# Third convolution: offset taps from TensorE to VectorE, turned values copied by ScalarE

## The reference

```
q   = dwconv3x3(x, stride 1)                       # queries, 16x16
k   = dwconv3x3(x, stride 2)                       # keys, 8x8
v   = dwconv3x3(x, stride 1)                       # values, 16x16
off = dwconv3x3(x, stride 2)                       # offsets, 8x8
off = gelu(layernorm(off) * ln_g + ln_b)
pos = tanh(reference points + w_off2 @ off)        # one (y, x) for each of 64 positions
v'  = bilinear samples of v at pos                 # 64 values
out = w_out @ attention-like product of q, k and v' (scores are not normalised by a softmax)
x   = x + out
```

## Time and profile before

| | |
|---|---|
| device time, median of three runs | 1309.3 us |
| device time of the profiled execution | 1304.56 us |
| span of the profiled execution | 1302.5 us, mean granted TensorE clock 0.947 |
| TensorE matmul (PE) busy | 1172.8 us, 90% |
| TensorE weight load (PEld) busy | 1019.4 us, 78% |
| VectorE (DVE) busy | 808.1 us, 62% |
| ScalarE (ACT) busy | 483.3 us, 37% |
| GpSimd (POOL) busy | 251.7 us, 19% |
| L1613, value taps | 64 operations, 64.6 us |
| L1781, query taps | 144 records, 66.5 us |

### The profile page before, as it was taken

The page is one execution under the profiler, slowest core; times in us unless marked ns, Lnnn a source line. Parts: engine busy times, 40 slices in busy tenths (PEclk is TensorE's granted clock), DMA queues, the critical chain, the costliest instruction groups (busy, mean ns, idle before and its releaser), DMA issues. The chain is left out here.

```text
span 1302.5 us, 23938 instructions
## 1 busy us (share of the span) xinstructions
PE 1172.8 (90%) x8436; PEld 1019.4 (78%) x8436; DVE 808.1 (62%) x2931; ACT 483.3 (37%) x944; POOL 251.7 (19%) x233
## 2 busy tenths in 40 slices
PE   2979999957999999999999999999999997997776
PEld 1968888946999998888897767678888986886455
DVE  6136676746667664666675676655767667677556
ACT  3524333313555553333332223233333322232452
POOL 3002212122010100311121343332121213111200
PEclk9989999977999999999998999999999999999677
DMA  3301000010000000000000000000000000000000
GB/s 134 83 9 62 17 30 19 1 49 1 2 2 1 2 1 2 1 1 0 0 1 1 2 2 1 2 2 1 2 0 0 1 1 1 1 1 4 1 10 36
DMA packets 11561, 15.67 MB, mean 12 GB/s; under 512 B 7385, under 2 KB 9007, under 8 KB 11346
## 3 DMA queue, kind: packets, MB, share of 16 engines
q1 hardware_dynamic: 10754, 12.86, 3.1%
q10 hardware_dynamic: 720, 1.66, 0.3%
HBM read 11.37 MB, written 3.15 MB: 11 GB/s over the span
## 5 line engine op out<-in xcount | busy, mean ns | idle before, releaser
L943 PEld LDWEIGHTS moe_dn<-all_w,moe_hid 128*128 128x128 f32 x2304 | 269.9, 192 | 5.4
L943 PE MATMUL moe_dn<-all_w,moe_hid 128*128 128x96 f32 x2304 | 271.7, 275 | 0.0
L878 ACT ACTIVATE moe_hid<-moe_up 128x512 f32<-128x512 f32 x288 | 169.9, 599 | 230.8 <-PE moe_up L935 218.3
L933 PE MATMUL moe_up<-front_xh,front_w1h 97*128 97x512 f32 x288 | 122.0, 424 | 0.7 <-PEq L1474 0.4
L935 PE MATMUL moe_up<-front_xl,front_w1h 97*128 97x512 f32 x288 | 113.7, 395 | 0.0
L827 DVE SCALAR_TENSOR_TENSOR all_X<-moe_dn,front_gate,all_X 128x96 f32 (+1 forms) x384 | 95.2, 310 | 29.4 <-PE moe_dn L943 24.6
L934 PE MATMUL moe_up<-front_xh,front_w1l 97*128 97x512 f32 x288 | 113.1, 393 | 0.0
L819 DVE SCALAR_TENSOR_TENSOR all_X<-all_b,front_gate,all_X 128x96 f32 (+1 forms) x384 | 102.6, 329 | 14.0 <-DVE all_X L827 7.6
L1371 PE MATMUL l1c_o<-l1c_vs,l1c_pt 128*128 128x64 f32 x768 | 94.4, 277 | 0.5 <-DVE l1c_ro L1149 0.5
L1371 PEld LDWEIGHTS l1c_o<-l1c_vs,l1c_pt 128*128 128x128 f32 x768 | 91.8, 195 | 2.9 <-issue 0.9
L1115 DVE TENSOR_REDUCE l1c_nmax<-l1c_sc 128x2 f32<-128x512 f32 x96 | 61.8, 686 | 40.1 <-PE l1c_sc L1338 39.4
(11 more groups left out here) (393 smaller groups left out, 2038.8 us busy)
## 6 DMA issues: line engine op xcount, KB each, us to landing
all_w<-w SPq DMA_DIRECT2D x3, 582.0 KB
all_w<-w SPq DMA_DIRECT2D x3, 576.0 KB
all_X<-x_rows SPq DMA_DIRECT2D x2, 768.0 KB, 6.9
conv_scratch<-all_X SPq DMA_DIRECT2D x2, 768.0 KB, 3.2
all_X<-conv_scratch SPq DMA_DIRECT2D x2, 768.0 KB, 4.9
out_tokens<-l3f_y SPq DMA_DIRECT2D x5, 288.0 KB, 2.1
l0c_band<-band ACTq DMA_DIRECT2D x1, 1248.0 KB, 9.4
all_b<-b SPq DMA_DIRECT2D x3, 192.0 KB
```

Of the source, the lines that this page charges most:

```text
L878: act.activation(hid[:, n, :], up[n % UPS][:, :], ACT.Gelu).then_inc(hid_done, 1)
L933: pe.matmul(bank, w1h[:, n, :], xh[:, p, :], start=True, stop=False)
L943: last = pe.matmul(dn[e % 2][:, j * C:(j + 1) * C], hid[:, n, j * P:(j + 1) * P], w2[:, n, :], start=(k == 0), stop=(k == KC - 1))
```

## The change

The nine offset taps go from TensorE to VectorE. They read `xp` at stride two in rows and columns, for both images at once: 17 rows of 8 elements, 136 elements in 96 partitions; the row between the two images is of no use. Tap 0 is a `tensor_scalar` with factor and bias, taps 1 to 8 are `scalar_tensor_tensor` operations with the running sum as second input, each waiting for the one before. TensorE turns the result by two ordinary matmuls with the identity (64 positions each) in place of one transpose. This turn now stands after the keys' taps and the turn of the values. VectorE's copy of the turned values is made by ScalarE, after the two score copies. `diag` has two kinds left of three, so GpSimd makes one fewer in the stage before. Keys and queries stay on TensorE.

```diff
-        self.diag = s.sb("diag", [C, 3, KS * KS, C])
+        self.diag = s.sb("diag", [C, 2, KS * KS, C])
...
-        for w in (2, 1, 0):
+        for w in (1, 0):
...
-        off = s.sb("off", [C, KP2])
+        off = s.sb("off", [C, KROWS, KSIDE])
...
+            def offset_taps(p, lo, hi):
+                if lo == 0:
+                    wait(dve, S["xp_done"], p + 1)
+                    wait(dve, S["on_in"], p)
+                for t in range(lo, hi):
+                    dy, dx = t // KS, t % KS
+                    rows = xp[:, p % 2, dy:dy + 2 * KROWS - 1:2, dx:dx + SIDE:2]
+                    if t == 0:
+                        ins = dve.tensor_scalar(off[:, :, :], rows, taps[:, 2, 0:1], bias[:, 2:3], ALU.mult, ALU.add)
+                    else:
+                        ins = dve.scalar_tensor_tensor(out=off[:, :, :], in0=rows, scalar=taps[:, 2, t:t + 1],
+                                                       in1=off[:, :, :], op0=ALU.mult, op1=ALU.add)
+                    if t < TAPS - 1:
+                        chain.sync(ins)
+                    else:
+                        ins.then_inc(S["off_done"], 1)
...
             for p in range(NP + 2):
+                if live(p):
+                    offset_taps(p, 0, 5)
                 if live(p - 2):
                     add_output(p - 2, 0)
                 if live(p):
-                    value_taps(p, 1, 5)
+                    offset_taps(p, 5, TAPS)
+                    value_taps(p, 1, 4)
                 if live(p - 2):
                     add_output(p - 2, 1)
                 if live(p):
                     offset_moments(p)
-                    value_taps(p, 5, 6)
+                    value_taps(p, 4, 6)
                     offset_norm(p)
-                if live(p - 1):
-                    values_out(p - 1)
...
-            def offsets_out(p):
-                wait(act, S["off_in"], p + 1)
-                wait(act, S["on_in"], p)
-                act.activation(off[:, :], off_ps, ACT.Identity, bias=bias[:, 2:3]).then_inc(S["off_out"], 1)
+            def values_out(p):
+                wait(act, S["vt_in"], p + 1)
+                wait(act, S["vb_in"], 2 * p)
+                act.activation(vt[:, :, :, :].rearrange("p i t c -> p (i t c)"), vp[:, 0:4 * C], ACT.Copy
+                               ).then_inc(S["vt_out"], 1)
...
                 if live(p - 1):
                     scores_out(p - 1, 0)
                     scores_out(p - 1, 1)
+                    values_out(p - 1)
...
-            def conv_offsets(p):
-                wait(pe, S["xp_done"], p + 1)
-                wait(pe, S["th_done"], p)
-                conv(off_ps, 2, p, 2, 0, TAPS).then_inc(S["off_in"], 1)
...
             def turn_offsets(p):
-                wait(pe, S["off_out"], p + 1)
-                pe.transpose(on_ps, off[:, :], ident[0:C, 0:C]).then_inc(S["on_in"], 1)
+                wait(pe, S["off_done"], p + 1)
+                wait(pe, S["th_done"], p)
+                for i in range(2):
+                    o = off[:, PAD // 2 * i:PAD // 2 * i + KSIDE, :].rearrange("c y x -> c (y x)")
+                    ins = pe.matmul(on_ps[KPIX * i:KPIX * (i + 1), :], o, ident[0:C, 0:C], start=True, stop=True)
+                ins.then_inc(S["on_in"], 1)
...
             for p in range(NP + 1):
-                if live(p):
-                    conv_offsets(p)
                 if p == NP - 1:
+                    pe.wait_ge(S["xp_done"], NP)
                     F.pe_turn(pe)
...
                 if live(p):
-                    turn_offsets(p)
                     conv_keys(p)
...
                 if live(p - 1):
                     turn_values(p - 1)
                 if live(p):
+                    turn_offsets(p)
                     conv_queries(p, 0, 4)
```

More of the change, by code:

```diff
@@ L1469, in l2_conv @@
     ROWS = PAD + SIDE
+    KROWS = PAD // 2 + KSIDE
     BATCHES = ((0, 8), (8, 20), (20, NT))
@@ L1500, in l2_conv @@
         k_ps, y_ps = ky[0:C, 0:KP2], ky[:, KP2:KP2 + 2 * C]
-        off_ps, on_ps, og_ps, pos_ps = fp[0:C, 0:KP2], fp[:, KP2:KP2 + C], fp[0:C, KP2 + C:KP2 + C + P], fp[:, 0:2 * KP2]
+        on_ps, og_ps, pos_ps = fp[:, 2 * KP2:2 * KP2 + C], fp[0:C, 2 * KP2 + C:2 * KP2 + C + P], fp[:, 0:2 * KP2]
         vb_ps = vb[0:BLK, 0:4 * C]
         names = ("tap_done", "var_done", "rstd_done", "dve_step", "xn_done", "turned",
-                 "xp_done", "off_in", "off_out", "on_in", "ovar_done", "orstd_done", "on_done", "og_in", "og_out",
+                 "xp_done", "off_done", "on_in", "ovar_done", "orstd_done", "on_done", "og_in", "og_out",
                  "pos_in", "th_done", "dist_done", "hat_done", "bil_done", "val_done", "vt_in", "vt_out", "k_in", "k_out",
@@ L1618, in value_taps @@
                         ins.then_inc(S["val_done"], 1)
[L1620 to L1624, removed]
             def sampled_out(p, i):
@@ L1743, in _ @@
             for p in range(NP + 1):
-                if live(p):
-                    offsets_out(p)
                 if p == NP - 1:
@@ L1783, in conv, with conv_keys @@
                 return ins
-            def conv_offsets(p):
+            def conv_keys(p):
                 wait(pe, S["xp_done"], p + 1)
-                wait(pe, S["th_done"], p)
-                conv(off_ps, 2, p, 2, 0, TAPS).then_inc(S["off_in"], 1)
-            def conv_keys(p):
                 wait(pe, S["k_out"], p)
```

## The result

| | before | after |
|---|---|---|
| device time, median (range, runs) | 1307.79 us (1304.84 to 1318.88, 4) | 1341.95 us (1337.88 to 1343.05, 4) |
| ratio, with its 95% interval | | 1.0239 (1.0195 to 1.0283) |
| span of the profiled execution | 1302.5 us | 1336.0 us |
| mean granted TensorE clock | 0.947 | 0.923 |
| length of the stage | 189.1 us | 224.0 us |

A forecast was written before the change was run, and what follows sets the result against it. TensorE was taken to set the stage's pace; waits on VectorE after the move summed over eight pairs to +15.8 us, giving 1320.4 from the profiled execution or 1325.1 from the median, stated as 1323, range 1303 to 1337.

The forecast's parts named there:

- the rival on the clock: TensorE's gaps drop its clock to the lower level: two to three us more a pair, 20 in all; chance 0.05.
- Taps of 0.36: Each of nine offset taps on VectorE lasts 0.36 us, 0.39 start to start, 3.5 us a pair.
- the rival of half rate: Stride-two reading makes each VectorE offset tap take 0.53 us: 10 us more, 1330 to 1335; chance 0.10.
- The turn, 0.37: Turning the offsets on TensorE by two ordinary float32 matmuls takes 0.37 us a pair, before 0.14.
- Step 1: Second projection waits for five taps and first add; starts 2.9 us after X, end of ScalarE's padded-image copy.
- Step 2: Keys wait for VectorE's second add, starting 7.3 us after ScalarE's padded-image copy, before 6.3; loss 1.0 us.
- Steps 3 and 4: Queries start 10.3 us after ScalarE's padded-image copy; second sampling group waits for masking until 18.9 to 19.0, loss 0.8.
- Step 5: From the second sampling group to ScalarE's next padded-image copy's end nothing changes: 5.67 us.
- Pair 1: Second pair of the stage: TensorE reaches second sampling before VectorE, and keys' blocks come late; +2.1 us.
- Pair 0: First pair of the stage: no adds in the way, turn back about 708.7 instead of 710.82; -2.1 us.
- Pair 7: Last pair: later queries and the next stage's front delay VectorE's masking and the second sampling group; +3.8 us.
- The first rival: TensorE stays the bound in the stage: 16.8 us less, 2.10 a pair, 1288 to 1292; chance 0.10.

The follow-up runs named there:

- e5: Changed kernel with unread matmuls filling TensorE's waits ahead of the second projection, the keys' taps and the first pair's turn back; 1319.76 us, ratio 1.0071.
- e6: Kernel before, offset taps still on TensorE, only the first add moved behind four value taps on VectorE; 1337.78 us, ratio 1.0218.
- e8: Changed kernel with adds earlier, value taps later, GpSimd's later statistics behind the keys' blocks, second projection between the two images' scores; 1290.48 us, ratio 0.9839.
- e9: Kernel before, offset taps still on TensorE, with value taps later and GpSimd's later statistics behind the keys' blocks; 1309.42 us, ratio 0.9996.
- e1: Changed kernel with nine unread matmuls in TensorE's wait ahead of the second projection, pairs 2 to 7; 1331.09 us, ratio 1.0135.
- e2: Changed kernel with VectorE's first add behind one offset tap instead of five, the second behind four offset taps; 1312.32 us, ratio 1.0001.

## Why the prediction was wrong

The differences to the kernel before, pair by pair in us (X to X; pair 0 from ScalarE's first tap to the first X, pair 7 from the last X to the end of the stage):

| pair | 0 | 1 | 2 | 3 | 4 | 5 | 6 | 7 | sum |
|---|---|---|---|---|---|---|---|---|---|
| forecast | -2.1 | +2.1 | +1.4 | +4 | +2.2 | +2.2 | +2.2 | +3.8 | +15.8 |
| e5 (clock up but in pair 1) | -2.2 | +3.7 | +1.3 | +3.8 | +1.8 | +1.7 | +1.6 | +2.6 | +14.3 |
| after | -0.6 | +1.8 | +5.0 | +3.8 | +8.1 | +5.3 | +3.8 | +7.8 | +34.9 |

**The step that failed** is the rival on the clock. Its mechanism and its price were there: gaps of 2.4 us near the start of each pair, 20 us in all. It got a chance of 0.05, "since groups of 3 us and more stand between the gaps", and the range left it out. The runs show those groups as the victims: the clock falls around the end of the gap, and the group of 3.01 us becomes one of 5.31. Measured by the difference of e5 and the kernel after, the price is 20.6 us; e6 shows the same fall with the gap alone. With that rival as the forecast the number would have been 1309.3 + 15.8 + 20 = 1345, against 1342. That its 20 us meet the 20.6 is in part luck: it had two to three us in each pair, and the rows for e5 and after differ by -1.9 (pair 1) to +6.3 (pair 4).

The sentence drawn from the Trainium skill beside it ("TensorE: Matmul & The Clock Gate", section Why this matters for your kernels), which warns of idle gaps between bursts of matmuls, is borne out in kind by the rows at 854.5 to 861.3; but the gaps that it names are longer than the 2.0 to 2.3 us that were enough here.

The reason given against the rival had no row under it, and one row of the kernel before spoke against it. Behind its front that stage has no gap over 1 us, but at the front a gap of 1.69 us was followed, from 701.3 on, by 6.8 us at the lower level, all that the stage had. The timeline shows the gap, and the busy times of its first stretch have the clock at 0.83:

```profile
699.34 2.82 PE L1781 MATMUL l2c_fp<-third_xp,third_diag 96*96 96x128 f32 x18 [1.69 <-ACTq L1741]
```

```profile
697.00:717.00 20.00, 17.14 (x70) 11.06 (x69) 11.28 (x40) 4.79 (x11) 5.41 (x4) 0.83 0.00 1
```

**Taps of 0.36.** Right. 64 of them have a median of 365 ns, tap 0 has 409, four start to start in 1.53 - 0.37 = 1.16, 0.39 each. Reading at stride two costs nothing that the line through the earlier trace rows doesn't give; the rival of half rate is out.

**The turn, 0.37.** Right: 864.26 to 864.58 is 0.32.

**Step 1**, projection at X + 2.9: it starts at 855.12, X + 2.9. One tap did wait for the bilinear product: four taps took 1.89 instead of 1.53, 0.36 for the reckoned 0.45.

**Step 2**, keys at X + 7.3: the add ends at X + 6.9 in the kernel after, and at the full clock (e5) the keys start at X + 7.1. In the kernel after they start at X + 9.2, by the slow scores.

**Steps 3 and 4.** In e5 the queries start at 850.98, X + 10.2 (forecast 10.3), and the second sampling group at 859.25, X + 18.5 (forecast 19.0, half a microsecond too much). TensorE waits there 0.30 to 0.46 us in pairs 4 to 6, for the forecast 0.8.

**Step 5.** 878.49 - 872.85 = 5.64 (forecast 5.67).

**Pair 1** was under-priced: 2.1 for a measured 3.7 in e5. The keys' blocks were named, but as something that VectorE meets; in e5 TensorE itself waits 4.5 us for them ahead of the scores, and the clock is at the lower level for 6.8 us there. How the 1.6 us divide between the two isn't shown. In the kernel after, pair 1 starts later, waits 2.8 us and has +1.8. **Pair 0** gained what was said in e5; in the kernel after its wait of 1.64 us ahead of the turn back was followed by a fall of the clock, and 0.6 was left. **Pair 7**: 2.6 in e5 for the forecast 3.8; the kernel after has 5.2 more, with 17.1 us at the lower level.

**The first rival** (TensorE stays the bound, 16.8 us less) was rightly refused for this order of work. Its price was a quarter too high: e8, where nothing waits in pairs 2 to 6, has pairs shorter by 1.6 us for the reckoned 2.10, and a stage shorter by 12.8 for the 16.8 (14.9 against e9). In pair 1 TensorE still stands for 2.7 us ahead of the turn. Of the 0.5 us that a steady pair lacks, 0.24 lie in projection and scores (3.46 us before, 3.70 in e8) and 0.12 from the keys to the queries (3.15 for the reckoned 3.03).

**Left open**: why a gap of 2.0 us brings the clock down in some pairs of e6 and not in others; why the last pair of e1 fell to the lower level at 897.0, behind gaps of 1.7 and 0.6 us that left the clock of e5 up; and what e5's fillers cost by themselves (its 14.3 us hold them, and the 6.8 us at the lower level in pair 1, so the waits alone may be a little less).

## What to carry to other kernels

Taking work from the busiest engine wins only what that engine doesn't then spend waiting: ask of each removed stretch what it hid, and place the new work behind everything that the relieved engine waits for (here the place of two adds in VectorE's list was worth 31 us). A wait of 2 us on TensorE in a stage that ran without gaps must be priced twice, once as itself and once as the matmuls behind it at the lower clock. Look for the nearest gap in the trace and read the granted clock behind it (here 1.69 us at the stage's front); if there is none, that case belongs into the range. Where the clock is in question, fill the gap with matmuls that nobody reads: what that gives back is the clock's share, what is left is the wait.

## What the hardware showed unexpectedly

- In the kernel after a gap of 2.3 us in pairs 2, 5 and 6 went with 7 to 10 us at the lower clock, and in pair 4, behind the same gap, and in pair 7, behind one of 1.9, it was 17 us each. In e6 a gap of 2.0 us went with 6.8 and 3.4 us in pairs 2 and 5 and with none in pairs 4 and 6. A gap of 0.57 us in each of pairs 4 to 6 of e2 left the clock at 1.00.
- A gap can be filled with work of no use at a profit: e1 and e5 add 0.24 us of matmul for each filler (2.20 us for nine of them) and are 11 and 22 us faster than the kernel after by the medians.
- GpSimd and two-input operations of VectorE exclude each other in small pieces too: the Trainium skill ("SBUF — State Buffer", section Who interferes with whom) calls it an exclusive lock of the shared port, and the traces agree: one offset tap of 0.37 us lasted up to 1.69 while GpSimd worked.
